# Flamingo gated block on one core: x read channel-major for the query projection, its normalisation moved into the scores

## What is computed

```python
Q = (layernorm(x) @ W_q.T)            # heads of 32
K = ctx @ W_k.T ; V = ctx @ W_v.T
s = Q K^T / sqrt(32) - slope[h] * (query_pos - key_pos)      # mask: -inf where it is 0
e = exp(s - max(s)) ; attn = e / (1 + sum(e))
x = x + tanh(g_xattn) * (attn V) @ W_o.T
xn = layernorm(x) ; xr, xk = mu * xn + (1 - mu) * xn_previous
x = x + tanh(g_ffn) * sigmoid(xr @ W_r.T) * (relu(xk @ W_k.T)^2 @ W_v.T)
```

## Time and profile before

| what | value |
|---|---|
| three runs, median | 1474.18 us |
| the profiled execution, its own time | 1474.89 us |
| its span, first to last instruction | 1473.1 us |
| PE busy (matmuls) | 1372.3 us, 93% of the span |
| VectorE, ScalarE, GpSimd busy | 1128.0, 891.0, 720.5 us |
| DMA | 65.97 MB, mean 45 GB/s |
| granted TensorE clock | 0.998 |

### The profile page before, as it was taken

The page is one execution under the profiler, slowest core; times in us unless marked ns, Lnnn a source line. Parts: engine busy times, 40 slices in busy tenths (PEclk is TensorE's granted clock), DMA queues, the critical chain, the costliest instruction groups (busy, mean ns, idle before and its releaser), DMA issues.

```text
span 1473.1 us, 34107 instructions
## 1 busy us (share of the span) xinstructions
PE 1372.3 (93%) x11584; PEld 1143.7 (78%) x11584; DVE 1128.0 (77%) x2745; ACT 891.0 (60%) x2928; POOL 720.5 (49%) x766
## 2 busy tenths in 40 slices
PE   7988999999999999999999999999999999999988
PEld 6876778778787877878787787878787787878767
DVE  5447868787887878788786879878687878878675
ACT  5247475665747476674747566574756657474752
POOL 0003555645555554555555465545556455555542
PEclk9999999999999999999999999999999999999999
DMA  8721002020100102011010201111010201101000
GB/s 270 220 80 38 26 17 64 0 53 26 49 29 28 50 0 79 0 49 29 28 50 14 64 0 49 29 40 39 28 51 0 64 15 49 29 28 42 3 29 29
DMA packets 53010, 65.97 MB, mean 45 GB/s; under 512 B 23024, under 2 KB 29168, under 8 KB 52976
## 3 DMA queue, kind: packets, MB, share of 16 engines
q1 hardware_dynamic: 52976, 65.52, 14.9%
HBM read 40.87 MB, written 24.64 MB: 44 GB/s over the span
## 4 chain that ended last, share of the span: by engine, by line
PE 36%; DVE 28%; issue 17%; POOL 9%; ACT 6%; DMA 2%; DVEq 1%; SPq 0%; POOLq 0%; ACTq 0%
PE rotating L417 26%; DVE diff L1144 4%; DVE probs_room L1082 4%; DVE mix_k L1136 4%; POOL probs_room L1362 4%; PE score_bank L417 3%; PE probs_bank L584 3%; ACT probs_room L824 3%; POOL norm L1400 2%; DVE relu L1144 2%; PE attn_bank L598 2%; DVE stats L1049 2%; DVE norm L1061 2%; DVE xs L1105 2%; POOL mixed_gate L1395 1%
## 5 line engine op out<-in xcount | busy, mean ns | idle before, releaser
L824 ACT ACTIVATE probs_room<-probs_room 128x121 f32<-128x121 f32 x1024 | 392.1, 388 | 28.5 <-DVE probs_room L1086 28.5
L1362 POOL TENSOR_TENSOR probs_room<-probs_room,recip 128x960 f32<-128x960 f32 x128 | 229.7, 1795 | 209.4 <-DVE recip L1094 209.4
L417 PE MATMUL rotating<-w_proj,attn_t 128*128 128x512 f32 x768 | 207.6, 409 | 21.0 <-ACT gated L875 19.0
L1082 DVE SCALAR_TENSOR_TENSOR probs_room<-mask_in,score_bank 128x120 f32<-128x120 f32 x1024 | 212.9, 270 | 3.3 <-issue 0.3
L417 PE MATMUL rotating<-mixed_key,w_key 128*128 128x256 f32 x1440 | 198.5, 289 | 11.0 <-ACT gated L875 11.0
L417 PE MATMUL rotating<-w_value,xnt_or_act 128*128 128x512 f32 x720 | 202.7, 410 | 6.4 <-DVE xs L1105 6.4
L831 ACT COPY probs_room<-probs_bank 120x512 f32<-120x512 f32 x256 | 150.0, 586 | 82.0 <-PE probs_bank L584 80.4
L417 PE MATMUL rotating<-xnt_or_act,w_query 128*128 128x256 f32 x1536 | 198.8, 286 | 0.5 <-DVE xnt_or_act L1067 0.5
L417 PEld LDWEIGHTS rotating<-mixed_key,w_key 128*128 128x128 f32 x1440 | 178.6, 191 | 22.0 <-ACT gated L875 17.3
L824 ACT ACTIVATION_READ_ACCUMULATOR probs_room<-probs_room 128x1 f32 x1024 | 195.0, 190 | 0.0
L417 PEld LDWEIGHTS rotating<-xnt_or_act,w_query 128*128 128x128 f32 x1536 | 187.8, 191 | 1.9 <-DVE xnt_or_act L1067 0.8
(11 more groups left out here) (121 smaller groups left out, 2109.7 us busy)
## 6 DMA issues: line engine op xcount, KB each, us to landing
xs<-in_x_dram SPq DMA_DIRECT2D x64, 256.0 KB, 2.9
out_dram<-gated SPq DMA_DIRECT2D x64, 256.0 KB, 3.0
value_scratch<-gated SPq DMA_DIRECT2D x16, 240.0 KB, 2.7
mask_in<-in_mask_dram SPq DMA_DIRECT2D x16, 240.0 KB, 3.3
keys_t<-key_scratch SPq DMA_DIRECT2D x16, 240.0 KB, 2.6
values<-value_scratch SPq DMA_DIRECT2D x16, 240.0 KB, 4.2
probs_room<-in_ctx_t_dram SPq DMA_DIRECT2D x6, 480.0 KB, 7.4
key_scratch<-query_t SPq DMA_DIRECT2D x12, 240.0 KB, 4.9
```

The source lines that it names most:

```text
L417: mm = pe.matmul(bank, stationary(a, c), moving(b, c), start=(i == 0), stop=(i == MATMULS - 1))
L824: e = act.activation(row, row, ACT.Exp, bias=neg_max[:, t % 2, head:head + 1], scale=-1.0, accum_out=sums[:, t % 2, head:head + 1])
L1082: z = dve.scalar_tensor_tensor(out=probs[:, t % 2, head, :], in0=far, scalar=-SLOPES[head], in1=score_banks[j][:, g * NK:(g + 1) * NK], op ...
L1362: pool.tensor_tensor(part, part, recip[:, t % 2, heads].unsqueeze(2).to_broadcast((P, H // 2, NK)), ALU.mult)\
```

## The change

`x` comes a second time from the host, transposed per batch (`x_t`, channel by token), and is loaded in two halves of 256 tokens straight into a raw buffer in the place of the normalised tile (the slots that the squared relu also uses). `turn1`, `turn1_out`, `turn1_low` and `normalise1` go; `xt_split` (ScalarE) and `xt_rest` (VectorE) make the two parts of raw x from SBUF, two instructions of 128x1024 on each engine. Since x is not normalised, the query weights lose their column means in the prologue (four float32 products with a matrix of 1/512 and four subtractions), and rstd is the scalar of the bias operation. The slopes move: keys are scaled by 1/(sqrt(32) slope) when they are made, and the exp multiplies by the slope. So one instruction adds the distance for four heads (128x480), the maximum follows as before, and `exp_biases` (VectorE, 128x8) makes the exp's bias for eight heads at once; `exps` wait for that. `attend` waits for all four `probs_out` of its tile. SyncE gets two loads per round and one wait for each. The list `ATTENTION_AND_FFN` loses one entry, `turn1` of tile 1, so all entries behind it change bank.

```diff
@@ the list of products, bank = place modulo 2 @@
-    ("value", 2, -1), ("gate", 3, -1), ("proj", 2, 0), ("turn1", 1, 1), ("value", 3, -1), ("proj", 3, 0),
-    ("query", 0, 1), ("query", 1, 1), ("query", 2, 1), ("query", 3, 1),
+    ("value", 2, -1), ("gate", 3, -1), ("proj", 2, 0), ("value", 3, -1), ("proj", 3, 0), ("query", 0, 1),
+    ("query", 1, 1), ("query", 2, 1), ("query", 3, 1),
@@ SyncE @@
+            def load_xt(b, half):
+                tokens = slice(half * S // 2, (half + 1) * S // 2)
+                sp.dma_start(raw_xt[:],
+                             x_t[bass.ds(b, 1), :, tokens].rearrange("b (c p) t -> p (b c) t", p=P))\
+                    .then_inc(xt_loaded[half], 16)
...
             for t in range(QT):
                 load_x(0, t)
+            for half in range(2):
+                tokens = slice(half * S // 2, (half + 1) * S // 2)
+                sp.dma_start(first_xt[:, :, tokens], x_t[0, :, tokens].rearrange("(c p) t -> p c t", p=P))\
+                    .then_inc(xt_loaded[half], 16)
             load_mask(0)
...
                 for t in range(QT):
                     if ffn:
+                        if t == 0 and not last:
+                            sp.wait_ge(act_low, b * CT)
+                            load_xt(b + 1, 0)
                         sp.wait_ge(out_ready, (b - 1) * QT + t + 1)
                         if not last:
                             load_x(b + 1, t)
                         store_out(b - 1, t)
+                    if t == 2 and not last:
+                        sp.wait_ge(xt_ready, b * 2 + 3)
+                        load_xt(b + 1, 1)
@@ PE, prologue: behind the first chunk @@
             chunk(0, 0, True)
+            pe.wait_ge(constants, 1)
+            pe.wait_ge(raw_weight[0], 32)
+            for c in range(CT):
+                mm = pe.matmul(probs_bank[:], mean_of[:], xs[:, 0, c], start=(c == 0), stop=(c == CT - 1))
+            mm.then_inc(mean_done, 1)
             chunk(0, 1, False)
@@ ScalarE @@
             def weight(i):
-                act.wait_ge(raw_weight[i % 2], 16 * (i // 2 + 1))
+                if i == 2:
+                    act.wait_ge(centred, 1)
+                else:
+                    act.wait_ge(raw_weight[i % 2], 16 * (i // 2 + 1))
...
+            keys_out(0, 0, True)
             weight(2)
-            keys_out(0, 0, True)
...
+            def xt_split(b, half):
+                tokens = slice(half * S // 2, (half + 1) * S // 2)
...
+                act.wait_ge(xt_loaded[half], b * 16 + 16)
+                act.copy(xnt_or_act[:, HI, :, tokens], raw_xt[:]).then_inc(xt_high, 1)
...
-                act.wait_ge(max_ready, (b * QT + t) * G + g + 1)
+                act.wait_ge(max_ready, (b * QT + t) * 2 + j // 2 + 1)
+                for g in groups:
+                    place = j * G + g
+                    row = probs_and_one[:, t % 2, place, :]
+                    e = act.activation(row, row, ACT.Exp, bias=exp_bias[:, t % 2, place:place + 1],
+                                       scale=SLOPES[g * J + j], accum_out=sums[:, t % 2, place:place + 1])
...
                 attn_out(b, 3)
-                after((turn1_out, 1))
-                after((turn1_out, 2))
+                after((xt_split, 0))
                 after((query_out, 0))
                 turn2_out(b, 2)
-                after((turn1_out, 3))
+                after((xt_split, 1))
                 after((query_out, 1))
@@ VectorE @@
+                dve.scalar_tensor_tensor(out=probs[:, t % 2, places, :], in0=score_banks[j][:, 0:G * NK]
+                                         .rearrange("p (g k) -> p g k", g=G), scalar=rstd1[:, t:t + 1], in1=far,
+                                         op0=ALU.mult, op1=ALU.add).then_inc(scores_biased, 1)
+                dve.wait_ge(scores_biased, (b * QT + t) * J + j + 1)
+                dve.tensor_reduce(top[:, t % 2, places], probs[:, t % 2, places, :], AX.X, ALU.max).then_inc(top_ready, 1)
+
+            def exp_biases(b, t, half):
+                places = slice(half * H // 2, (half + 1) * H // 2)
+                dve.wait_ge(top_ready, (b * QT + t) * J + half * 2 + 2)
+                dve.tensor_tensor(exp_bias[:, t % 2, places], top[:, t % 2, places], neg_slopes[:, places], ALU.mult)\
+                    .then_inc(max_ready, 1)
...
                 bias(b, 3, 0)
                 bias(b, 3, 1)
-                after((normalise1, 0))
+                exp_biases(b, 3, 0)
                 bias(b, 3, 2)
                 residual(b, 1)
                 statistics2(b, 1)
                 reciprocals(b, 3, 0)
                 bias(b, 3, 3)
+                exp_biases(b, 3, 1)
...
                 attn_low(b, 3)
-                after((turn1_low, 1))
-                after((normalise1, 2))
+                after((xt_rest, 0))
                 statistics2(b, 2)
                 feed_forward((finish, 3))
                 normalise2(b, 2)
                 residual(b, 3)
-                after((turn1_low, 2))
                 after((statistics1, 3))
                 statistics2(b, 3)
-                after((normalise1, 3))
                 normalise2(b, 3)
-                after((turn1_low, 3))
+                after((xt_rest, 1))
                 mix_key(b, 1)
@@ VectorE, prologue, ahead of the splits of weights 2 to 6 and of values_out(0, 0) @@
+            dve.wait_ge(mean_done, 1)
+            for c in range(CT):
+                m = dve.tensor_tensor(xs[:, 0, c], xs[:, 0, c], probs_bank[:], ALU.subtract)
+            m.then_inc(centred, 1)
             weight(2)
             weight(3)
             values_out(0, 0, True)
```

More of the change, by code:

```diff
@@ L713, in _ @@
             pe.wait_ge(ident_ready, 1)
-            first = [u for u in ATTENTION_AND_FFN if u[0] in ("turn1", "query")]
-            for t in range(QT):
-                turn1(0, t, None).then_inc(done["turn1"], 1)
+            first = [u for u in ATTENTION_AND_FFN if u[0] == "query"]
             for u in range(4):
@@ L1245, in batch @@
                 mix_gate(b, 0)
-                after((turn1_low, 0))
-                after((normalise1, 1))
                 after((statistics1, 2))
```

199 lines of the change are left out of this document (95 added, 104 removed).

## The result

The changed kernel takes 1553.5 us (median of four, 1552.7 to 1555.6) against 1473.6 (1472.7 to 1476.5) for the kernel before: 1.054 times as long, 95% interval 1.052 to 1.056. The prediction was 1529 with a range of 1486 to 1556: the direction was right, the loss of 80 us was forecast as 55, and the time lies near the upper end of the range.

The account below looks back on a forecast made before the run. PE was taken as the bound, the change costed along a VectorE, ScalarE and PE loop: 1473.1 + 16.4 + 38.5 - 1 + 1 = 1528 of span, 1529.8 with 1.8 around it; less 0.7 for the profiled execution, 1529, range 1486 to 1556.

Parts of the forecast that it names:

- So PE is the bound: Whole round: PE, busy 79.9 of 84.61 us, bounds it; less PE work should shorten it if no other engine comes late.
- The exps' wait: Tile 3, key(3) to attend(3): first exp 1.25 us later, attend(2) 2.25 later, end of attend(3) 1.85 later.
- Attend(3) to gate(0): End of attend(3) to the next gate(0): 23.25 us against 21.35, +1.9 per round, with gate(0) waiting for query_out(3).
- So mix_gate(2) sets the piece: Attend(3) to gate(0): the wait takes back PE's 1.3 us gain, so mix_gate(2), ending 16.55 us after finish(3), sets the length.
- rival (b): x of tile 3 is no part of the chain; a round costs +0.5 us, 1498 in all; chance 0.15.
- Gate(0) to key(3): Head of the round: idle before key(0) and scores(1) closes, turned probabilities wait longer; 22.28 becomes 21.3 us, -1.0.
- a term of 0.55: Gate(0) to key(3): added because late exps push GpSimd's second normalise_probs and PE's idle of 0.74 and 0.71 grows to some 2.0.
- (c): Rival: the gap before gate(0) lowers the clock, 1.5 us lost on two gates, 0.5 to 1.5 staying; 1536 to 1550; chance 0.15.
- (e): Rival: xt_rest(1) meets GpSimd's difference(2) on the shared port, 0.8 us longer per round; 1540; chance 0.10.
- Prologue: Before the first query: query weights' split 14.7 us late behind the mean product, plus x_t loads and clock; +16.4 (11 to 22).
- Batch 0: First batch: no finish and no wait for x of tile 3, -1 us.
- the round's 2.75: Sum per round of 1.85 + 1.9 - 1.0 us; 14 rounds +38.5; bounds +0.3 to +4.2.

Follow-up runs that it names:

- b_defer: Kernel before, with only mix_gate(3) and its ScalarE and GpSimd parts moved into the next round behind reciprocals(0,0): 1442.3 us (0.979).
- b_half: Kernel before, with only the exps of four heads waiting for the minima of all eight heads of their half: 1512.4 us (1.026).
- a_exps4: Changed kernel, with exp_biases run per four heads behind each bias and exps waiting for their own four: 1519.7 us.
- a_order: Changed kernel, with bias(3,3) and its exp_biases ahead of residual(1), statistics2(1) and reciprocals(3,0) on VectorE: 1522.5 us.
- a_banks: Changed kernel, with the rotating banks of the kernel before, so gate(0) no longer waits for query_out(3): 1553.7 us.
- b_banks2: Kernel before, with only the banks of query(2) and query(3) swapped, so gate(0) waits for the eviction of query(3): 1484.9 us (1.009).
- a_stats: Changed kernel, with statistics1(3) behind statistics2(3) on VectorE, and rstd1 behind rstd2 of tile 3 on GpSimd: 1540.1 us.
- a_nocentre: Changed kernel without the centring of the query weights (mean product, subtractions and the split's wait left out): 1540.1 us.

## Why the prediction was right, and where its steps were off

**The bound.** "So PE is the bound" was wrong, although the text went on to cost the loop and not the busy time; that choice is why the sign came out. b_defer shows it.

**The exps' wait: right in mechanism and place, too small.** bias(3,3) behind the reciprocals, the exps of half a tile behind it, attend(2) late: rows 955.55 to 959.07 show the sequence as forecast, and b_half, a_exps4 and a_order each move the time by 31 to 38 us. Counted from key(3), attend(2) came 2.93 us later (32.93 for 30.00), not 2.25. Of the 0.68 missing, 0.20 are in the first exp (25.10 us after key(3), not 24.90), 0.18 in ScalarE's exps up to the reciprocals, and 0.33 in the step from reciprocals to exps (2.13, not 1.8): `exp_biases` took 0.58 there, beside GpSimd's normalise_probs(3,0), where I had 0.3 with its wait. The 1.12 ahead of the second turn is the same delay of the first exp. The fused bias, estimated at 0.65, has 0.704 in the mean.

**Attend(3) to gate(0): about the size, for the wrong reason.** 23.77 against 21.35 is +2.42, and I had +1.9. The chain came as forecast: finish(3) ended 5.44 us after attend(3) (5.55 forecast), mix_gate(2) 17.05 after that (16.55), and gate(0) started 1.28 later (1.15). But a_banks and b_banks2 show the wait of gate(0) to be slack. The step that failed is "So mix_gate(2) sets the piece": the time that PE spends there comes off again between gate(0) and key(3), so this piece is no term of its own. What counts is VectorE's queue up to bias(0,0), and there the 2.01 us for x of tile 3 and xt_rest(1) at 2.06 use up what the change had freed. a_stats recovers 13.4 of it, 19.0 beside mended exps, where xt_rest(1) and (0) shrank by only 12.6 in all (52.2 to 39.6 us). So the wait for x does count, which speaks against rival (b).

**Gate(0) to key(3): right in size**, 21.21 for the predicted 21.3; but the loop's +1.34 in front of tile 0 is hidden in it. That the two pieces together came near, +1.35 for the predicted +0.9, is in part luck: the wait that +1.9 was built on costs nothing, and of the losses that count the one at tile 0 had a term of 0.55 and the wait for x of tile 3 had none.

**Rivals (c) and (e) both happened.** (c) The clock falls behind the gap at gate(0), to 0.77 in the mean over the gates of 904.93, and there it cost next to nothing, as a_banks shows. It costs elsewhere: four of 14 rounds are 89.7 to 90.2 long. In three of them the gate of tile 3 takes 3.8 to 4.6 us instead of 3.0, as at 1314.22 below (granted clock 0.63); in the fourth the first two gates take 8.63 (0.64). These rounds are 0.4 us of the mean.

```profile
1314.22 4.61 PE L451 MATMUL rotating<-w_gate,mixed_gate 128*128 128x512 f32 x12
```

(e) xt_rest(1) takes 2.06 where xt_rest(0) takes 1.22, the 0.8 us that was named. In a_stats it shrank together with the load's wait, so its price by itself stays open.

**Prologue: right**, +13.9 for +16.4. The mean product takes 3.59 (estimate 3.6), chunk five stands at 71.63 (forecast not before 70), and a_nocentre gives 11.1 of the shift to the centring, where the forecast had 14.7.

**Batch 0 was mis-sized**, +4.8 where I had −1. I left out two things of about the same size. Its tiles wait for their exps like all others: attend(2) stands behind 1.45 us of idle that was not there before, and up to attend(0) there are 1.1 us more. And products ran at a lower granted clock: the first queries take 13.22 us for 11.78 (0.87 in the mean), and the stretch from turn2 to the end of the product behind it 4.9 for 3.4 (150.74 to 155.66, 0.68).

In sum the round's 2.75 was 4.3; in the prediction's own pieces 0.7 more from key(3) to attend(3), 0.5 from there to gate(0), 0.4 from the clock. 14 times that are 22 of the 24 us missed; batch 0 adds 5.8, and the prologue and the end give 2.5 and 0.9 back.

## What to carry to other kernels

In a loop over several engines, the busy shares don't say who sets the round: follow each engine's written order and look for the step that stands in a queue ahead of something urgent without being urgent itself; moving mix_gate(3) gained 2.1 us per round, where 1.8 us of transposes taken from PE showed no gain while these waits stood. When two small steps are merged into one (minima of eight heads for four), what waits for the first half now waits for both, and that is paid on the tile with no lead. Work taken out from beside a load turns into a wait for the load, if the load's issue doesn't come earlier too.

## What the runs showed of the hardware

In these rows a VectorE instruction with two SBUF inputs is as long as its neighbour on GpSimd lets it be. Of after, the length of `exp_biases` (minimum, median, maximum in ns), and GpSimd beside the two slow rows shown above:

```profile
L1113 DVE TENSOR_TENSOR exp_bias<-probs_room,neg_slopes x128: 166/203/739, 117.6 to 1490.8; 128x8 f32<-128x8 f32 x128
```

```profile
955.84 1.79 POOL L1400 TENSOR_TENSOR probs_room<-probs_room,recip 128x960 f32<-128x960 f32 x1 [0.48 <-DVE recip L1121]
...
981.57 1.25 POOL L1421 TENSOR_TENSOR diff<-xn2t 128x512 f32<-128x512 f32 x1
```

The 0.58 of 957.06 ends at 957.64, with GpSimd's product (957.63); the xt_rest of 981.84 ends 1.08 us after GpSimd's (982.82 to 983.90), which is about the 1.22 that it takes alone. Of the 128 `exp_biases` of after, the 64 that begin while no product of two tensors runs on GpSimd take 0.17 us, and the 64 that begin while one runs end 0.01 to 0.04 us behind it. That fits a wait for the whole rest of GpSimd's instruction, even for an operation of 0.17 us. The Trainium skill ("SBUF — State Buffer", Who interferes with whom) states this rule, and these rows agree with it. Behind the wait both kinds need some 0.15 us less than they take alone, so part of the operation seems to run under it (an inference).

The granted clock fell behind gaps of 1.86 to 2.35 us ahead of gate(0) in some rounds and not in others of the same gap: in b_banks2 the same gates took 5.71 us at 1.00 behind 1.86, and 7.32 at 0.77 behind 1.89. The first queries of batch 0 stand behind 2.48 to 2.49 us of idle in all nine executions of changed kernels; in five of them they took 13.2 us, in four 11.75. What decides was not settled.
